# Destinations of a tile computed one unit earlier, and accumulating DMAs for the closing sum

## The reference

```
logits = x @ Wr * 256**-0.5                       # 8 experts
_, idx = top_k(logits + rb, 2)
w = softmax(take_along_axis(logits, idx))
h = (x @ W1[e]) * silu(x @ W3[e]);  expert_out = h @ W2[e]      # for the two chosen e
out = sum over the two of w * expert_out
out = out + ((x @ Ws1) * silu(x @ Ws3)) @ Ws2     # the shared expert
x = layernorm(x + out)
```

## Time and profile before

| | us |
|---|---|
| median of three runs | 3486.91 |
| the profiled execution itself | 3485.83 |
| its span | 3483.7 |
| busy: PE / DVE / POOL / ACT | 2999.7 / 2530.5 / 1674.7 / 1449.3 |
| first routed unit's last `lo` (unit 16, DVE line 1932) starts | 2873.96 |
| the same of the last unit (54) | 3425.26 |

### The profile page before, as it was taken

One profiled execution on the slowest core, in us unless ns is written; L12 is line 12 of the kernel. 1 busy time (PEld: TensorE's weight loads), 2 busy tenths in 40 slices (PEclk: granted clock), 3 DMA queues, 4 the chain that ended last, 5 costly groups with the idle time before them and its releaser, 6 DMA issues. The chain is left out here.

```text
span 3483.7 us, 52943 instructions
## 1 busy us (share of the span) xinstructions
PE 2999.7 (86%) x17256; PEld 2171.2 (62%) x17256; DVE 2530.5 (73%) x3858; ACT 1449.3 (42%) x2076; POOL 1674.7 (48%) x1186
## 2 busy tenths in 40 slices
PE   6999999698889889889898898988987897777773
PEld 4888888555546545555554554554554897777773
DVE  3555545687897897888888779878877647766666
ACT  2222222354445445445445444544543333333333
POOL 2222222265574565566557556655654343444445
PEclk9999999899999999999999999999998998888886
DMA  8000100200100100100100100100101324444445
GB/s 236 13 14 14 22 18 13 55 25 16 41 25 19 44 19 25 44 13 25 44 18 19 50 13 19 53 15 20 49 13 59 110 71 143 146 144 147 143 138 177
DMA packets 137039, 197.69 MB, mean 57 GB/s; under 512 B 16992, under 2 KB 96864, under 8 KB 136736
## 3 DMA queue, kind: packets, MB, share of 16 engines
q1 hardware_dynamic: 115696, 160.52, 15.7%
q10 hardware_dynamic: 14224, 14.58, 1.6%
q0 software_dynamic: 6816, 18.75, 1.4%
HBM read 118.54 MB, written 41.71 MB: 46 GB/s over the span
## 5 line engine op out<-in xcount | busy, mean ns | idle before, releaser
L1082 ACT ACTIVATE raw<-b_ps 128x1024 f32<-128x1024 f32 x512 | 505.4, 1021 | 460.6 <-PE b_ps L854 385.6
L1226 DVE TENSOR_SCALAR raw<-raw 128x1024 f32<-128x1024 f32 x512 | 578.2, 1135 | 117.5 <-ACT raw L1082 115.5
L965 PE MATMUL b_ps<-raw 128*64 128x512 f32 x2048 | 510.2, 620 | 113.9 <-DVE raw L1226 113.2
L853 PE MATMUL b_ps<-b_QQ,b_KT 128*128 128x512 f32 x1024 | 436.7, 426 | 15.6 <-DMA b_QQ<-b_QQ 8.6
L823 POOL TENSOR_TENSOR b_acc<-b_acc,raw 128x512 f32<-128x512 f32 x256 | 373.0, 1457 | 86.1 <-DVE raw L1226 54.2
L854 PE MATMUL b_ps<-b_QQ,b_KT 128*128 128x512 f32 x1024 | 407.0, 397 | 0.0
L827 POOL TENSOR_TENSOR b_acc<-b_acc,raw 128x512 f32<-128x512 f32 x256 | 388.7, 1518 | 20.1
L806 POOL TENSOR_TENSOR b_QQ<-raw,b_QQ 128x512 fp32r<-128x512 f32 x128 | 165.3, 1291 | 404.5 <-ACT b_QQ L1032 404.5
L1678 PE MATMUL c_ps<-c_xT_l,c_w_h 128*128 128x256 f32 x1504 | 359.1, 322 | 0.0
L965 PEld LDWEIGHTS b_ps<-raw 128*64 128x64 f32 x2048 | 126.3, 138 | 371.2 <-issue 196.8
L853 PEld LDWEIGHTS b_ps<-b_QQ,b_KT 128*128 128x128 f32 x1024 | 195.2, 191 | 247.8 <-issue 188.5
(11 more groups left out here) (262 smaller groups left out, 7268.5 us busy)
## 6 DMA issues: line engine op xcount, KB each, us to landing
c_raw<-in_L_ffn_W_dram SPq DMA_DIRECT2D x117, 512.0 KB, 5.4
b_QQ<-b_QQ SPq DMA_DIRECT2D x128, 256.0 KB, 3.7
xs<-zeros ACTq DMA_DIRECT2D x1, 10140.0 KB, 67.9
c_xg<-xs SPq DMA_DIRECT2D x39, 260.0 KB, 2.7
b_rows<-in_ctx_dram SPq DMA_DIRECT2D x9, 1024.0 KB, 7.5
a_xt<-in_x_dram SPq DMA_DIRECT2D x72, 64.0 KB, 2.2
b_rows<-x SPq DMA_DIRECT2D x9, 512.0 KB, 7.1
x<-a_x1t SPq DMA_DIRECT2D x64, 64.0 KB, 1.9
```

The costliest lines, as they stand in the source:

```text
L853: pe.matmul(bank(key, a), k, QQ[:, n % 2, hh, 0, :], start=True, stop=False)
L965: mm = pe.matmul(bank(key)[hh * HD:(hh + 1) * HD, :], V[:, t, (2 * p + hh) * HD:(2 * p + hh + 1) * HD], probs[:, at_step(j, hh), (t % 2) * ...
L1082: ins = act.activation(probs[:, at_step(j, hh), :], both(key), ACT.Exp, scale=SCALE)
L1226: dve.tensor_scalar(pr, pr, HI, LO, ALU.min, ALU.max).then_inc(clipped, 1)
```

## The change

`goals` moves and changes its form. Before, `goals(j)` came at the end of unit 16 + j. Now `goals(j + 1)` comes within that unit, right after `lo(u, 0)`, that is, behind the DVE instruction which makes the low part of the rows of tile j + 1 that PE has just turned. Since the destinations are made earlier, `goal_u` and `share` get four buffers in place of two, and the wait for the send that last used the `yr` buffer moves from `goals` into `take`. Three of its eight instructions take another form: `tensor_scalar` becomes `scalar_tensor_tensor` with a constant tile (`nought`, `second_at`) as the second operand. The closing sum's second half no longer passes through `other` and POOL's addition: POOL issues two DMAs for each chunk which add the second choices' rows to what `dense[c]` holds in SBUF.

```diff
@@ -1388,11 +1387,13 @@
         token_u = sb("c_token_u", [P, NT], U32)
         posf = sb("c_posf", [P, 2, NT])
         posu = sb("c_posu", [P, 2, NT], U32)
-        share = sb("c_share", [P, 2, 3, TT])
+        share = sb("c_share", [P, 4, 3, TT])
         goal = sb("c_goal", [P, 4, TT])
+        nought = sb("c_nought", [P, TT])
+        second_at = sb("c_second_at", [P, TT])
         hole_u = sb("c_hole_u", [P, TT], U32)
         hole = sb("c_hole", [P, TT])
-        goal_u = sb("c_goal_u", [P, 2, TT], U32)
+        goal_u = sb("c_goal_u", [P, 4, TT], U32)
         mhalf = sb("c_mhalf", [P, CT])
         st = sb("c_st", [P, CT, 6])
         mv = sb("c_mv", [P, 2, CT, 2])
@@ -1461,6 +1461,13 @@
 
         def logit_bank(c):
             return ps[:, 7 - 2 * (c % 2), (c // 2) * CT * E:(c // 2 + 1) * CT * E]
+
+        def joined(c):
+
+            n = 32 * (c // 3 + 1)
+            if c % 3 == 2:
+                return scattered, 16 * 2 * NT + n
+            return sent[c % 3], 16 * TT * ((TILES + 1 - c % 3) // 2) + n
 
         def results(half, c):
             return ys[half * SECOND + 1 + c * 512:half * SECOND + 1 + (c + 1) * 512].rearrange("(t p) d -> p t d", p=P)
@@ -1571,7 +1580,7 @@
                     pool.wait_ge(y_drained, DENSE + j + 1)
                     for t in range(TT):
                         pool.indirect_dma_start(
-                            out=ys[:, :], out_offset=bass.IndirectOffsetOnAxis(ap=goal_u[:, j % 2, t:t + 1], axis=0),
+                            out=ys[:, :], out_offset=bass.IndirectOffsetOnAxis(ap=goal_u[:, j % 4, t:t + 1], axis=0),
                             in_=yr[:, j % 2, t, :], in_offset=None).then_inc(sent[j % 2], 16)
 
                 split_lo(1)
@@ -1584,8 +1593,16 @@
                 send(TILES - 1)
 
                 def both(c):
-                    pool.wait_ge(x_in[c], 48)
-                    pool.tensor_tensor(dense[c], dense[c], other[c], ALU.add).then_inc(pooled, 1)
+
+                    if c >= 3:
+                        pool.wait_ge(*joined(c - 3))
+                    pool.wait_ge(x_in[c], 32)
+                    if c < 3:
+                        for k in range(2):
+                            pool.wait_ge(sent[k], 16 * TT * ((TILES + 1 - k) // 2))
+                    for t in (slice(0, 2), slice(2, 4)):
+                        pool.dma_start(dense[c][:, t, :], results(1, c)[:, t, :],
+                                       accum_op=ALU.add).then_inc(joined(c)[0], 16)
 
                 def root(c):
                     pool.wait_ge(var_ready, c + 1)
@@ -1777,12 +1794,6 @@
                         cast(n, 2)
                     silu(u, 1)
                     hi(u, 1)
-                for k in range(2):
-                    act.wait_ge(sent[k], 16 * TT * ((TILES + 1 - k) // 2))
-                for m in range(2):
-                    wait_split(act, SETS - 1, m)
-                for c in range(CH):
-                    act.dma_start(other[c], results(1, c)).then_inc(x_in[c], 16)
                 for c in range(CH):
                     act.wait_ge(shift_ready, c + 1)
                     for t in range(c * CT, (c + 1) * CT):
@@ -1880,21 +1891,21 @@
 
                 def goals(j):
 
-                    k = j % 2
+                    k, q = j % 2, j % 4
                     dve.wait_ge(xg_in[k], 16 * (j // 2 + 1))
-                    if j >= 2:
-                        dve.wait_ge(sent[k], 16 * TT * (j // 2))
+                    if j >= 4:
+                        dve.wait_ge(sent[k], 16 * TT * (j // 2 - 1))
                     own = owner[:, j:j + 1]
-
-                    link(dve.tensor_scalar(goal[:, 2, :], hole[:, :], float(j * T), None, ALU.add))
                     eid, token = xg[:, k, :, EID], xg[:, k, :, TOKEN]
-                    dve.scalar_tensor_tensor(share[:, k, 0, :], eid, own, xg[:, k, :, SHARE], ALU.is_equal, ALU.mult)
-                    dve.scalar_tensor_tensor(share[:, k, 1, :], eid, own, xg[:, k, :, SHARE + 1], ALU.not_equal, ALU.mult)
-                    dve.tensor_scalar(goal[:, 0, :], eid, own, float(SECOND), ALU.not_equal, ALU.mult)
-                    link(dve.scalar_tensor_tensor(goal[:, 1, :], token, 0.0, goal[:, 2, :], ALU.is_equal, ALU.mult))
+
+                    dve.scalar_tensor_tensor(goal[:, 2, :], hole[:, :], float(j * T), nought[:, :], ALU.add, ALU.add)
+                    dve.scalar_tensor_tensor(goal[:, 0, :], eid, own, second_at[:, :], ALU.not_equal, ALU.mult)
+                    dve.scalar_tensor_tensor(share[:, q, 0, :], eid, own, xg[:, k, :, SHARE], ALU.is_equal, ALU.mult)
+                    link(dve.scalar_tensor_tensor(share[:, q, 1, :], eid, own, xg[:, k, :, SHARE + 1], ALU.not_equal, ALU.mult))
+                    dve.scalar_tensor_tensor(goal[:, 1, :], token, 0.0, goal[:, 2, :], ALU.is_equal, ALU.mult)
+                    dve.tensor_tensor(share[:, q, 2, :], share[:, q, 0, :], share[:, q, 1, :], ALU.add)
                     link(dve.tensor_tensor(goal[:, 3, :], goal[:, 0, :], token, ALU.add))
-                    dve.tensor_tensor(goal_u[:, k, :], goal[:, 3, :], goal[:, 1, :], ALU.add)
-                    dve.tensor_tensor(share[:, k, 2, :], share[:, k, 0, :], share[:, k, 1, :], ALU.add).then_inc(goals_ready, 1)
+                    dve.tensor_tensor(goal_u[:, q, :], goal[:, 3, :], goal[:, 1, :], ALU.add).then_inc(goals_ready, 1)
 
                 def take(u):
 
@@ -1905,9 +1916,11 @@
                     else:
                         j = u - DENSE
                         dve.wait_ge(goals_ready, j + 1)
+                        if j >= 2:
+                            dve.wait_ge(sent[j % 2], 16 * TT * (j // 2))
                         for t in range(TT):
                             ins = dve.tensor_scalar(yr[:, j % 2, t, :], src[:, t * D:(t + 1) * D],
-                                                    share[:, j % 2, 2, t:t + 1], None, ALU.mult)
+                                                    share[:, j % 4, 2, t:t + 1], None, ALU.mult)
                     ins.then_inc(y_drained, 1)
 
                 def add_dense(c):
@@ -1946,14 +1959,14 @@
                         dve.tensor_tensor(xr[j % 2][1], ps[:, 6 + j % 2, :].rearrange("p (k n) -> p k n", k=KD),
                                           xr[j % 2][0].bitcast(F32), ALU.subtract).then_inc(xl_ready, 1)
                     lo(u, 0)
+                    if nxt:
+                        goals(u + 1 - DENSE)
                     if u == 0:
                         places()
                     if u >= DENSE:
                         split_lo(weight_set(u), 2)
                     product(u, 1)
                     lo(u, 1)
-                    if u >= DENSE:
-                        goals(u - DENSE)
                     if DENSE + 2 <= u < DENSE + 2 + CH:
                         add_dense(u - DENSE - 2)
                 take(UNITS - 2)
@@ -1969,7 +1982,7 @@
                 def combine(c):
 
                     k = c % 2
-                    dve.wait_ge(pooled, c + 1)
+                    dve.wait_ge(*joined(c))
                     dve.wait_ge(dense_added, c + 1)
                     at = y[:, c * CT:(c + 1) * CT, 0:D]
                     chained(dve.tensor_tensor(at, at, dense[c], ALU.add))
```

More of the change, by code:

```diff
@@ L1355, in experts @@
         dense = [over("dense", c, 0) for c in range(CH)]
-        other = [raw[:, 0, c, :].rearrange("p (t d) -> p t d", d=D) if c < 2 else over("other", c, 1) for c in range(CH)]
         wr = sb("c_wr", [P, KD, E])
@@ L1438, in experts @@
         dense_added = sem("c_dense_added")
-        pooled = sem("c_pooled")
         var_ready = sem("c_var_ready")
@@ L1532, in _ @@
                 pool.memset(mhalf[:, :], -0.5).then_inc(consts, 1)
+                pool.memset(nought[:, :], 0.0).then_inc(consts, 1)
+                pool.memset(second_at[:, :], float(SECOND)).then_inc(consts, 1)
                 pool.memset(every[:, :], 1.0).then_inc(consts, 1)
@@ L1535, in _ @@
                 pool.memset(every_f[:, :], 1.0).then_inc(consts, 1)
-                pool.wait_ge(consts, 8)
+                pool.wait_ge(consts, 10)
                 pool.tensor_copy(lane[:, :], step_u[:, :]).then_inc(consts, 1)
-                pool.wait_ge(consts, 9)
+                pool.wait_ge(consts, 11)
                 pool.tensor_scalar(steps[:, :], lane[:, :], float(T), None, ALU.mult).then_inc(consts, 1)
@@ L1547, in _ @@
                 pool.tensor_copy(wrs[:, :, 0, :], wr[:, :, :]).then_inc(consts, 1)
-                pool.wait_ge(consts, 16)
+                pool.wait_ge(consts, 18)
                 pool.tensor_tensor(wrs[:, :, 1, :], wr[:, :, :], wrs[:, :, 0, :].bitcast(F32), ALU.subtract
@@ L1616, in logits @@
                     if c == 0:
-                        pe.wait_ge(consts, 17)
+                        pe.wait_ge(consts, 19)
                     else:
@@ L1833, in _ @@
                     link(tops(c))
-                dve.wait_ge(consts, 17)
+                dve.wait_ge(consts, 19)
```

## The result

The changed kernel takes 3347.49 us (median of 4 runs, 3343.3 to 3348.81) against 3486.72 (4 runs): ratio 0.9598, 95% interval [0.9582, 0.9615]. It is faster, as forecast, but 50 us slower than the 3297 forecast and outside the range of 3272 to 3332. Three stretches of the profiled execution tell where the time went.

A forecast was written before the change was run, and what follows sets the result against it. A loop of waits through `goals` and the row load bounds the routed units; cutting 551.3 us to 362.7 saves 188.6, all else 0: 3485.83 - 188.6 = 3297.2 us. Range 3272 to 3332; the forecast itself, 3285 to 3308, has 50%.

The forecast's parts named there:

- What bounds the kernel: Routed units: a loop of waits through `goals`, row load, PE's turn and 24 matmuls sets the pace, 14.51 us a unit.
- The period, 9.44 us led by DVE: Routed units after the change: DVE's own program takes 9.44 us a unit, PE's 9.07, so PE waits about 0.4.
- The row load lands in about 2.7 us: Routed units: gathered rows, asked for some two units before PE turns them, land in about 2.7 us, over 7 to spare.
- The new form, 0: `goals`: `scalar_tensor_tensor` in place of three `tensor_scalar` gains nothing, the place alone does; bounds 0 and 0.2 us.
- The moved wait, 0: `take(u)` waits for the send of two units before: 0 taken; the longest landing, 16.9 us, would cost 5 us once.
- the memsets, 0: Constants: two more memsets on POOL, long before PE waits for them, cost 0.
- The closing sum, "I take 0": After the last `lo`: accumulating DMAs change nothing from 58.4 us; bounds 6.4 saved and 11.5 lost, the latter a 13% rival.
- The slower rival: Closing sum: the 16 accumulating DMAs go one at a time, 16.9 us each; +206 us, 3503; chance 2%.
- PE-led rival, 9.07: Routed units: DVE's hold under POOL is shorter, so PE's 9.07 us sets the period; 206.6 saved, 3279 us; chance 22%.
- Port rival: Routed units: POOL's second subtraction gets in ahead of DVE's, costing 1.24 us a unit, 37 times; 3343 us; chance 7%.
- Clock rival: Routed units: PE's gaps keep 24 matmuls at 5.08 us, 11.27 a unit, 1.83 over DVE; 3365 us; chance 4%.
- Rows come no earlier: Routed units: SP's queue holds the row load back behind its weight loads, so nothing is gained; 3486 us; chance 2%.
- The signs: Profile marks: right, 9.1 to 9.5 us a unit, clock 1.00, no `c_xg` wait; wrong, chunks over 5 us apart.

## Why the prediction was wrong in its time, and where it was right

- *What bounds the kernel*: right. The loop through `goals` and the row load was the pace, and with it went PE's wait and the low clock (0.85 to 1.00).
- *The period, 9.44 us led by DVE*: right to 0.02, and step by step. From the `lo` on the forecast had the end of the held subtraction at 3.95, `product` at 3.86, the next `lo` at 5.24, the w2 subtraction at 6.92; the rows above give 3.96, 3.88, 5.31 and 6.95. Small misses cancel in it: the subtraction was held for 2.06 us and not 1.90, the `lo` came 0.07 later, `goals` took 1.03 and not 1.07. Moving the w3 subtraction away from POOL gained 0.2 us a unit, so DVE was the leader. The 362.7 us for the stretch were 361.4. Of the difference 0.9 is an error of the sum: it books unit 16's `goals` in this stretch, but they stand ahead of the `lo` that begins it, and are part of the +1.4 us of the first row of the table.
- *The row load lands in about 2.7 us*: it took 5.9 us in the median, beside the weights at 219 GB/s. The cover of over 7 us, worked out from its place, was enough: PE did not wait for the rows.
- *The new form, 0*: right, by both runs, though for two instructions and not three (1.000 in the old place; 507.5 against 507.8 us in the new). In the old place either form is held beside POOL's subtraction (2.2 us), in the new one neither is (0.20 and 0.25 us).
- *The moved wait, 0; the memsets, 0*: right. `take` follows its `lo` within 0.61 us in the rows above.
- *The closing sum, "I take 0", with 11.5 us as the upper bound*: this is the step that failed. It measured +51.8. The bound came from the rate of full DMA engines (12 MB at 357 GB/s), which supposes that enough DMAs are under way to fill them. While the chunks were added up they were not full: share 0.50 and 93 GB/s in the window above. One at a time, the term is a count times a landing: the 15 DMAs from 3259.39 to the last combine at 3336.28 take 76.9 us, which is 15 x 4.67 = 70 and some 7 for landings that took longer. Most of it lies in six landings, those of a chunk's second DMA from the third chunk on, 5.3 to 5.7 us from its issue to the combine (3278.07 to 3283.41 the first). Each time SP's store of a finished chunk begins just behind that DMA. The first such store, and the windows of a first DMA's landing, without a store, and of the second's, with one:

```profile
3278.64 0.38 SPq L1530 DMA_DIRECT2D out_dram<-c_y  x1
3273.60:3277.90 4.30, 0.00 (x0) 0.00 (x0) 2.80 (x11) 1.36 (x3) 1.03 (x1) 0.50 0.43 61
3278.20:3283.50 5.30, 0.00 (x0) 0.00 (x0) 0.09 (x1) 0.41 (x1) 2.18 (x2) 0.50 0.67 148
```

  The second chunk's second DMA, with no store beside it, landed in 4.37 us (3268.79 to 3273.16). That the store is what lengthens the landing was not tested by a run of its own. The bound's other guess, that an addition keeps the engines twice as long, came out near: 28.1% against 15.1% of the 16 engines' time. And with the room doubled and the look-ahead, so that the engines are nearly full (0.95), the new sum costs 11.9 us over the old one, close to the 11.5 of the bound; that the two agree so well is in part luck, since the bound counted the loads only, at the full 357 GB/s.
- *The slower rival had the mechanism*: accumulating DMAs one at a time. I priced it with the slowest load of a full queue, 16.9 us, and so put it at 3503 and 2%. A DMA that has the engines to itself is not in a full queue. The row for that was there: a load alone lands in 2.65 us. At that price the rival's own working gives 14 x 2.65 + 10.7 - 41 = +7 us, and with the 4.6 measured +34. The rest of the 51.8 are the first combine, which comes 9.5 us later, and some 8 by which 14 DMAs in 72.5 us are slower than 4.6 us each. Priced so, the rival would not have been "slower" but "less fast", with a real chance and up to some 3330, and the range would have had to reach beyond that. The sentence "two at once would keep below the 4.32 us a chunk" took for granted what was in question.
- The Trainium skill's fit ("DMA: Bandwidth & Descriptors", "Anatomy of one DMA — SWDGE (gpsimd) path") gave 2.6 us for each DMA of 256 KB; plain ones, two at a time, took 3.8 in the median (3.2 at the least) and accumulating ones 4.6. The measurement decides: even the plain ones gave 4.63 us a chunk, no less than the 4.32 of before.
- *PE-led rival, 9.07*: not met. *Port rival*: POOL's subtraction did not get in ahead. *Clock rival*: clock 1.00. *Rows come no earlier*: they did.
- *The signs*: of those for "right" all came but one. PE's short waits name no `sem_inc` behind `product`, but mostly "issue" (13.8 us) and the low part of the rows (`c_xT_l`, 4.3 us), so it is the run with the moved subtraction and not this sign that shows DVE as the leader. Of those for "wrong" one came: chunks over 5 us apart.

Open: how many bytes of descriptors an accumulating DMA of 256 rows needs. The runs say that in 1024 bytes one is under way, in 2048 up to three at first and about two in the steady state. As an estimate, if the room is simply filled up: over 512 bytes a partition, since two do not fit in 1024, and at most 683, since three fit in 2048; for a plain one at most 512, since two go at once in 1024. Larger room was not run.

## What to carry to other kernels

An upper bound from a full bandwidth is only a bound if something keeps the DMA engines full; ask how many DMAs can be under way, by buffers, semaphores and descriptor room, and price the case of one at a time with the landing of a lone DMA. When that limit is lifted, look at the share of the DMA engines again: here they were next. Where a change has two halves that touch different stretches, time each alone: here one gives 196 us and the other costs 52. When two kernels differ by a few us, compare the edited stretch in their traces and time them side by side on one chip; the same kernel gave 3286.28 us (0.9434 [0.9418, 0.945]) on one chip and 3293.46 us (0.9456 [0.9443, 0.9469]) on another.

## What was not expected of the hardware

- POOL stood still for 3.5 us between two DMA issues with no wait in the program; the profile calls it "issue". It changed with the descriptor room and with the size of the DMAs, and with plain DMAs it came only now and then between the two of a pair (0.36 to 0.56 us), and once, for 6.26 us, ahead of the second chunk's pair.
- A DMA of 256 rows of 1 KB that adds to SBUF: issue 1.23 us against 0.74, landing 4.6 us against 3.8, and 1.9 times the DMA engines' time for the same bytes (with it the queue's last sends, in both).
- POOL's root of 128x4 elements took 2.02 us in the kernel before while DVE was at work beside it, and 1.01 to 1.04 us where DVE was idle (the last `c_rs` of that kernel, and those in the runs with plain DMAs or more room).
